# The chain to the MLP's factors in two parts: 56 tiles inside the drain of phase 1, the last 8 tiles on GpSimd in small pieces during phase 2

## The reference

```
ada = cond @ w_ada + b_ada                 # shift, scale, gate, twice
xm  = expmap0(layer_norm(logmap0(x)) * (1 + sc_msa) + sh_msa)
q, k, v = heads(plin(xm, w_q)), ...        # plin(x) = expmap0(logmap0(x) @ w + b)
z   = plin(attention(q, k, v), w_o)
x1  = mobius_add(x, expmap0(g_msa * logmap0(z)))      # = ALPHA * x + BETA * zg
xm  = expmap0(layer_norm(logmap0(x1)) * (1 + sc_mlp) + sh_mlp)
ff  = plin(plin(xm, w_f1), w_f2)
out = x + mobius_add(x1, expmap0(g_mlp * logmap0(ff)))
```

## Time and profile before

| | |
|---|---|
| median of 3 runs | 765.38 us (765.11 to 765.99) |
| the profiled execution | 765.7 us, its span 763.9 us |
| busy over the span | PE 644.4 us (84%), DVE 654.1 (86%), ACT 524.7 (69%), POOL 347.0 (45%) |
| 500 to 520 us | PE 0.00 us busy, DVE 16.86, ACT 6.57, POOL 2.57; granted clock 0.50 |
| 640 to 700 us | PE 57.26 us busy, DVE 56.25, ACT 55.22, POOL 23.58; granted clock 1.00 |

### The profile page before, as it was taken

How to read it: one execution, slowest core, us unless ns; L and a number is a source line. 1 busy time by engine, 2 the same in 40 slices (tenths; PEclk the granted TensorE clock), 3 DMA queues, 4 the chain that set the end, 5 groups by cost and what they waited for, 6 DMA issues and landing times. The chain is left out here.

```text
span 763.9 us, 27111 instructions
## 1 busy us (share of the span) xinstructions
PE 644.4 (84%) x8419; PEld 464.3 (61%) x8433; DVE 654.1 (86%) x2171; ACT 524.7 (69%) x1563; POOL 347.0 (45%) x683
## 2 busy tenths in 40 slices
PE   4956889999999999999999997605669999999996
PEld 2645667777777777777777775402326566656664
DVE  2786788999999999999999997485998999999975
ACT  1123567777777777777777775334879989999874
POOL 1003556666666666666666665111234244234321
PEclk9978899999999999999999998656999999999999
DMA  9942876666666666666666665222444455445523
GB/s 321 359 116 57 141 131 137 146 141 143 141 147 142 145 142 147 141 141 144 147 140 147 144 133 113 50 70 70 124 124 133 139 158 163 149 132 166 164 72 110
DMA packets 184804, 107.50 MB, mean 141 GB/s; under 512 B 140188, under 2 KB 167591, under 8 KB 184744
## 3 DMA queue, kind: packets, MB, share of 16 engines
q1 hardware_dynamic: 182952, 103.99, 55.6%
q10 hardware_dynamic: 1792, 2.89, 1.0%
HBM read 64.11 MB, written 9.18 MB: 96 GB/s over the span
## 5 line engine op out<-in xcount | busy, mean ns | idle before, releaser
L885 PE MATMUL p_qkv<-wqkv,tT 128*128 128x256 f32 x768 | 198.1, 396 | 5.5 <-DVE u L1143 5.5
L885 PEld LDWEIGHTS p_qkv<-wqkv,tT 128*128 128x128 f32 x768 | 139.7, 195 | 22.9 <-issue 6.3
L899 PEld LDWEIGHTS p_o<-v,pT 64*64 64x64 f32 x4096 | 66.7, 136 | 21.9 <-issue 21.9
L899 PE MATMUL p_o<-v,pT 64*64 64x17 f32 x4096 | 73.0, 210 | 0.0
L858 PE MATMUL p_oz<-wo,oT 128*128 128x256 f32 x256 | 69.7, 397 | 0.0
L445 POOL TENSOR_TENSOR rt<-ss_t,c_mhalf 128x1 f32<-128x1 f32 x64 | 42.1, 658 | 60.6 <-ACT junk L634 53.7
L659 ACT ACTIVATE pT<-p_s 128x1024 f32<-128x1024 f32 x64 | 65.6, 1024 | 2.8 <-PE p_s L875 1.7
L1143 DVE SCALAR_TENSOR_TENSOR u<-p_qkv,ct,bqkv 128x768 f32<-128x768 f32 x64 | 64.3, 1005 | 3.5 <-PE p_qkv L885 3.5
L617 ACT ACTIVATE oT<-p_oz 128x256 f32<-128x256 f32 x64 | 24.6, 384 | 57.0 <-PE p_oz L850 57.0
L504 POOL TENSOR_TENSOR rt<-ss,c_mhalf 128x2 f32<-128x2 f32 x32 | 26.5, 827 | 80.8 <-ACT wqkv L707 80.8
L933 PE MATMUL p_t<-ident,pT 128*128 128x128 f32 x128 | 21.3, 290 | 46.5 <-ACT pT L714 46.5
(11 more groups left out here) (275 smaller groups left out, 1685.2 us busy)
## 6 DMA issues: line engine op xcount, KB each, us to landing
mod<-mod_rows SPq DMA_DIRECT2D x128, 128.0 KB, 2.9
x_all<-in_x SPq DMA_DIRECT2D x8, 1024.0 KB, 14.3
gate<-mod_rows SPq DMA_DIRECT2D x128, 64.0 KB, 2.7
mod<-mod_rows SPq DMA_DIRECT2D x32, 256.0 KB, 4.2
mod_b<-mod_rows SPq DMA_DIRECT2D x32, 256.0 KB, 4.4
out<-x_all SPq DMA_DIRECT2D x32, 256.0 KB, 3.0
gate<-gate_rows SPq DMA_DIRECT2D x32, 128.0 KB, 2.9
bqkv<-gate_rows SPq DMA_DIRECT2D x32, 128.0 KB, 2.9
```

What stands on the lines that cost most here:

```text
L885: mm = pe.matmul(p_qkv[:, a * D:a * D + D], tT[:, k, c, :], wqkv[:, c, a * D:a * D + D], start=c == 0, stop=c == C - 1)
L899: mm = pe.matmul(p_o[S * e:S * e + S, col:col + VW], pT[keys, e, g, :], v[keys, k, 2 * g + e, :], start=True, stop=True, skip_group_check= ...
```

## The change

The chain's code is put into functions of ten stages, which work on a slice of the columns. EARLY are tiles 0 to 55, LATE are the last 8.

- EARLY: DVE runs the stages inside slots 64 to 69 of phase 1, between `dot_x` and `gate_z`; ACT answers in its slots 65 to 70, POOL computes the moments in slot 69. Only the two first sums, `log_map_norm`, `scale_t2` and `scale_of_norm` stay behind phase 1. `split_ff_bias` moves from slot 69 to slot 66.
- LATE: POOL does all of it in phase 2, in slots 2 to 24, each piece before (`late_middle`) or after (`late_end`) its `token_roots2`. [...] Inverse roots and reciprocals are powers there. ACT answers with one Tanh in slot 7 and one Ln in slot 20, the latter between two table loads. DVE and ACT wait for `late_made` before pair 28.
- SP's waits for phase 1 move into the slots of phase 2 that need them.

```diff
+        EARLY, LATE = slice(0, T - 2 * GROUP), slice(T - 2 * GROUP, T)
+        LATE_TANH, LATE_LN = 7, 20
@@ SP, slot2
+                    if i == 1:
+                        sp.wait_ge(o_psum, T)
...
+                    if i == 0:
+                        sp.wait_ge(zg_ready, T)
+                        sp.wait_ge(u_ready, T)
...
-            sp.wait_ge(zg_ready, T)
-            sp.wait_ge(u_ready, T)
-            sp.wait_ge(o_psum, T)
@@ POOL, phase 1 slot
+                if isinstance(h, int) and 2 * h + off == T + 5:
+                    moments_of_sum()
@@ POOL, slot2
                 if on2(h, off, M_B):
                     inner_roots(slots - M_B)
+                late_middle(slots)
                 if group_at(h, off, M_N) is not None:
                     output_roots(group_at(h, off, M_N), parity(off, M_N))
                 if on2(h, off, M_A):
                     token_roots2(slots - M_A)
                 if group_at(h, off, M_N) is not None:
                     norm_roots(group_at(h, off, M_N))
+                late_end(slots)
+            def fused(dst, a, s1, b, f1_, f2_):
+                step(pool.tensor_scalar(late_tmp[:, :], a, s1, None, f1_))
+                step(pool.tensor_tensor(row(dst), late_tmp[:, :], b, f2_))
+            def power(dst, a, exponent):
+                step(pool.tensor_tensor(row(dst), row(a), exponent[:, :], ALU.pow))
+            def late_middle(n):
...
+                if n == 13:
+                    tt(Y0, ALPHA, MEAN, ALU.mult)
+                    tt(Y1, BETA, ZMEAN, ALU.mult)
+                    tt(MEAN1, Y0, Y1, ALU.add)
+                    tt(Y0, AA, VAR, ALU.mult)
...
+                if n == 21:
+                    tt(W10, W10, W4, ALU.mult)
+                    pool.wait_ge(late_answers, 2)
+                    fused(W8, row(W8), 0.5, row(W4), ALU.mult, ALU.mult)
...
+            def late_end(n):
...
+                if n == 13:
+                    tt(Y1, BB, ZVAR, ALU.mult)
+                    tt(Y0, Y0, Y1, ALU.add)
+                    tt(Y1, AB2, COV, ALU.mult)
+                    tt(VAR1, Y0, Y1, ALU.add)
...
+                if n == 24:
+                    tt(R2, W12, W4, ALU.mult)
+                    pool.drain().then_inc(late_made, 1)
@@ ACT, phase 1 slot, after evac_tT and before square_z
+                if isinstance(h, int) and 2 * h + off in (T + 1, T + 2):
+                    cols[0] = EARLY
+                    rsq()
+                if isinstance(h, int) and 2 * h + off == T + 3:
+                    act.preload_act_table_set("exp_and_others")
+                    elementwise(ACT.Tanh, W7, W8)
+                if isinstance(h, int) and 2 * h + off == T + 5:
+                    act.preload_act_table_set("natural_log_exp_and_others")
+                    rsq()
+                if isinstance(h, int) and 2 * h + off == T + 6:
+                    elementwise(ACT.Ln, W7, W8)
@@ ACT, slot2, before square_ff
+                if slots == LATE_LN:
+                    act.wait_ge(late_asks, 2)
+                    act.preload_act_table_set("natural_log_exp_and_others")
+                    act.activation(row(W8), row(W7), ACT.Ln).then_inc(late_answers, 1)
+                    act.preload_act_table_set("exp_and_others")
@@ DVE, phase 1 slot, after dot_x and before gate_z
-                if isinstance(h, int) and 2 * h + off == T + L_L - 1:
-                    split_ff_bias()
+                if s == T:
+                    cols[0] = EARLY
+                    dve.wait_ge(stats_kept, EARLY.stop)
+                    moments_of_z()
+                if s == T + 1:
+                    clipped_z()
+                if s == T + 2:
+                    split_ff_bias()
+                    norm_of_z()
+                if s == T + 4:
+                    sum_factors()
+                    dve.drain().then_inc(alpha_made, 1)
+                    squared_factors()
+                    dve.drain().then_inc(sums_made, 1)
+                    norm_of_sum()
+                if s == T + 5:
+                    log_map_argument()
+                    log_map_series()
@@ DVE, between the phases
-            dve.wait_ge(stats_kept, T)
...
             for j in range(2):
                 first_sum(0, j)
-            log_map_argument()
-            log_map_series()
             dve.wait_ge(moment_step, 8)
             log_map_norm(VAR1)
```

More of the change, by code:

```diff
@@ L160, in build @@
         c_tiny = sb("c_tiny", [P, 1])
+        c_mone = sb("c_mone", [P, 8])
+        late_tmp = sb("late_tmp", [P, 8])
         ff = qk[:, :].rearrange("p (j d) -> p j d", j=2)
@@ L686, in scale_x @@
                 n = 2 * i + j
+                if n == LATE.start:
+                    act.wait_ge(late_made, 1)
                 after(act, x1_ready, n - 1)
@@ L689, in scale_x @@
                                scale=arrays[:, ALPHA, bass.ds(n, 1)]).then_inc(xa_ready, 1)
-            rsq()
-            rsq()
-            elementwise(ACT.Tanh, W7, W8)
-            act.preload_act_table_set("natural_log_exp_and_others")
             act.wait_ge(alpha_made, 1)
@@ L697, in _ @@
                 scale_x(0, j)
-            rsq()
-            elementwise(ACT.Ln, W7, W8)
             rsq()
@@ L773, in slot2 @@
                     tanh_norm(group_at(h, off, M_P))
+                if slots == LATE_TANH:
+                    cols[0] = LATE
+                    act.wait_ge(late_asks, 1)
+                    act.activation(row(W8), row(W7), ACT.Tanh).then_inc(late_answers, 1)
+                if slots == LATE_LN:
[3 more added lines that the diff above has]
+                    act.preload_act_table_set("exp_and_others")
                 if on2(h, off, M_B):
@@ L779, in slot2 @@
                         square_fg(slots - M_B, j, (off - M_B) % TURN, q, col)
-            act.preload_act_table(ACT.Tanh)
+            act.preload_act_table_set("exp_and_others")
             act.wait_ge(factors_made, 1)
@@ L1036, in take_rsq, with fused, reciprocal @@
                 stt(dst, W3, 1.5, W2_, ALU.add, ALU.mult)
-            def log_map_argument():
-                take_rsq(W4)
-                tt(W5, W0, W4, ALU.mult)
-                ts(W5, W5, MAX_ARG, ALU.min)
-                ts(W6, W5, -1.0, ALU.mult, 1.0, ALU.add)
-                step(dve.reciprocal(row(W6), row(W6)))
-                stt(W7, W5, 1.0, W6, ALU.add, ALU.mult)
-                ask()
-            def log_map_series():
-                tt(W9, W5, W5, ALU.mult)
-                ts(W10, W9, 1.0 / 15, ALU.mult)
-                for m in (13, 11, 9, 7, 5, 3):
-                    stt(W10, W10, 1.0 / m, W9, ALU.add, ALU.mult)
-                stt(W10, W10, 1.0, W5, ALU.add, ALU.mult)
-                tt(W10, W10, W4, ALU.mult)
-            def log_map_norm(var):
-                take()
-                stt(W8, W8, 0.5, W4, ALU.mult, ALU.mult)
-                tt(W10, W10, W8, ALU.subtract)
-                stt(W10, W5, SERIES_BELOW, W10, ALU.is_lt, ALU.mult)
-                tt(W12, W8, W10, ALU.add)
-                tt(W0, W12, W12, ALU.mult)
-                stt(W0, var, 0.0, W0, ALU.max, ALU.mult)
-                ts(W0, W0, LN_EPS, ALU.add)
-                ask()
-            def scale_of_norm(dst):
-                take_rsq(W4)
-                tt(dst, W12, W4, ALU.mult)
+            def fused(dst, a, s1, b, f1_, f2_):
+                step(dve.scalar_tensor_tensor(out=row(dst), in0=a, scalar=s1, in1=b, op0=f1_, op1=f2_))
+            def reciprocal(dst):
+                step(dve.reciprocal(row(dst), row(dst)))
+            (moments_of_z, clipped_z, norm_of_z, sum_factors, squared_factors, norm_of_sum, log_map_argument, log_map_series,
+             log_map_norm, scale_of_norm) = boundary_stages(dve, step, tt, ts, stt, fused, reciprocal, ask, take, take_rsq)
             def tile_of(big, i):
@@ L1472, in slot2 @@
                     half = (TURN // 2) * h + (off - M_A) // 2
+                    if 2 * i == LATE.start:
+                        dve.wait_ge(late_made, 1)
                     for j in range(2):
```

280 lines of the change are left out of this document (216 added, 64 removed).

## The result

The changed kernel takes 756.53 us (median of four runs, 755.44 to 757.36) beside 765.25 us for the one before (four runs); the ratio is 0.9888, 95% interval 0.9868 to 0.9909. 757.8 us was forecast. The profiled execution took 756.48 us, its span is 754.4 us, 9.5 us shorter than before.

What follows compares the result with a forecast made beforehand. PE and DVE are over 90% busy in both phases; the chain between them costs latency. 765.7 - 10.8 (boundary) + 2.5 (Ln) + 0.7 (DVE beside POOL) = 758.1, median 0.3 lower: 757.8 us, range 753.5 to 763.0.

Steps and rivals of the forecast that it cites:

- What is removed: Between the last `gate_z` and the first `shift_t2`: 23.8 us shrink to 6.7, so 17.1 us go.
- Slots 65 and 66: Drain: chain pieces and bias, 6.7 us, exceed 3.76 idle by 2.95; with 0.25 for slot 64, 3.2 us late.
- The clock at 480: Slot 67: PE's clock falls to half already at 480 us, its work taking 5.1 against 3.2 us: 1.9 us.
- Slot 68: Drain: `sum_factors` to `norm_of_sum` take 6.5 us; with the slower PE ahead, 1.2 us are over the idle time.
- Slot 69: Drain: `log_map_argument` and `log_map_series` take 5.0 us where the bias was; 1.9 us over.
- The drain: End of phase 1: delays of 3.2, 1.2 and 1.9 make it 6.3 us longer; phase 2 starts 10.8 us earlier.
- The Ln on ACT: Phase 2, slot 20: two table loads and an activation stop ACT 2.8 us; 2.5 us were taken as the cost.
- POOL's pieces: Phase 2: 87 small pieces at 0.35 us each lie hidden in POOL's gaps before rt and rh.
- DVE beside POOL: Phase 2: 81 POOL pieces slow DVE by 0.7 us in all, 5.4 us as upper bound.
- Rivals 2 and 3: Phase 2: POOL's pieces too long, 763 us (chance 0.13); POOL takes the port from DVE, 770 us (chance 0.08).
- rival 3: Phase 2: POOL takes DVE's port, 770 us; by the skill's rule 23 us held in all; chance 0.08.
- Its own signs of being wrong: First `shift_t2` far from 509.7 us, or a turn of four slots longer between slots 8 and 24 than after.

Runs made afterwards that it cites:

- run 5: The changed kernel with the bias split (`split_ff_bias`) moved from slot 66 to slot 2 of the start: 751.89 us, ratio 0.9828.
- run 1: The changed kernel without the logarithm of slot 20, both table loads gone and the Ln made a Copy: 752.44 us, ratio 0.9828.
- run 3: The changed kernel with nine unread matmuls on PE ahead of its wait in `transpose_t2` of slot 21: 754.36 us, ratio 0.986.
- run 4: The changed kernel with none of the late work on POOL and ACT in phase 2, six memsets standing in: 753.48 us, ratio 0.9831.
- run 12: The kernel before, unchanged, traced a second time: one execution, 765.75 us.
- run 11: The changed kernel with seven Copies on ACT in place of slot 20's Ln and its table loads: 756.22 us, ratio 0.9896.
- run 8: The kernel before with only the bias split moved to slot 2 of the start: 762.53 us, ratio 0.9972.
- run 2: The changed kernel with the second table load moved two slots behind the Ln: 754.86 us, ratio 0.986.

## Why the prediction was right, and where not

The sign and the time (757.8 for 756.5 us) were right, inside the likeliest case; two terms of the sum were off and a third thing wasn't in it. That the total came out so near is in part luck, as the last point shows.

- *What is removed*: 17.1 us forecast, 23.8 - 6.4, 17.5 with all digits, measured. Right.
- *Slots 65 and 66*: 3.2 us forecast. The `gate_z` of slot 66 stood 9.85 us behind the u of tile 63 before (468.56 and 478.41), and stands 12.66 behind it now (463.46 and 476.12): 2.8. Right, with no idle time before it; in run 5 it stands 10.46 behind.
- *The clock at 480*: half level in slot 67, right, and so its price, 2.0 us for the 1.9. PE waited 3.54 us ahead of it where 4.05 had been forecast. That it is the late `gate_z`, and PE's longer wait with it, that brings the clock down isn't shown: in run 5 the gate is 2.2 us earlier, PE waits 1.27 us, and the clock falls as well. Here the result fits the forecast, and the mechanism stays open.
- *Slot 68*: 6.5 us of chain forecast, 6.44 measured (484.52 to 490.96). *Slot 69*: 5.0 forecast, 5.4 measured (492.28 to 497.68).
- *The drain*: 6.3 us longer forecast; from the u of tile 63 to the last `gate_z` it took 28.08 us and takes 34.22, 6.1. The boundary gained 11.3 us for 10.8.
- *"The Ln on ACT ... I take 2.5"*: the mis-sized term. It cost 5.8. The sum went from one row, ACT's own time, which was right (2.81), and stopped there. Behind ACT PE had to wait 2.9 us, and came back at half clock for some 6 us. I had used just this step for slot 67 and left it out for slot 20. Runs 1 and 3 show the two halves, 2.8 and 3.0 us. The Trainium skill ("ScalarE: Activation LUTs", What ACT_TABLE_LOAD costs), with its 2.66 us a switch, would have given an estimate of 5.6 for the piece, near the 5.8, but by another way, a drain with each switch. The rows have no such drain, each activation starts 0.01 us behind its load, and in run 3 the piece costs 2.8 with both loads in it.
- *POOL's pieces*: hidden, right (run 4); from start to start 0.28 us, and 0.39 beside DVE's operations with two inputs from SBUF, for the forecast 0.35. *DVE beside POOL*: 0.7 us forecast, about 0.2 measured (0.02 to 0.1 a turn, run 4). Rivals 2 and 3 are out. The rule of the Trainium skill ("SBUF — State Buffer", SBUF: two separate sides), under which rival 3 had its worst case, isn't seen on DVE: its two-input operations keep to 475 to 484 ns, beside powers of 1.76 us too. On POOL the rows fit it, 0.32 us for a piece beside these operations and 0.21 elsewhere: if one engine waits there, it is POOL. That it waits for the port is not shown by itself.
- *Its own signs of being wrong*: the first `shift_t2` was to be near 509.7 us and came at 504.05. Of those 5.6 us the 5.1 below are phase 1's, so counted from the u of tile 63 the sum of the drain held. The turn of slots 21 to 24 was 6 us longer than the later ones, which was the sign for rivals 2 and 3; run 1 shows that it was the logarithm. And the low end of the forecast's own bounds, added up from the four terms, is 754.1 us and not 755.5.
- *Not in the sum*: the 5.1 us by which phase 1, untouched but for slot 64, was ahead in the trace. They hid the 3.3 us of the logarithm and 0.9 us in slots 2 to 9.

Those 5.1 us are a matter of single executions, at least in good part. Across the thirteen other traces, in code that is the same but for the bias split and slot 64, the u of tile 63 starts anywhere from 461.9 to 467.6 us, and slots 2 to 9 take 54.2 to 57.2 us where no matmuls are added. The start differs in single windows, as these, of the changed kernel and then of run 12, show:

```profile
85.00:90.00 5.00, 4.11 (x67) 1.00 0.68 142
```

```profile
85.00:90.00 5.00, 3.44 (x43) 0.66 1.00 126
```

The low window is not the old program's: run 11, of the new one, has 0.66 in it too.

What stays open: by the traces the change is worth 11.3 - 5.8 = 5.5 us (4.6 with the boundary of run 12), by the medians 8.7, with an interval of 7.0 to 10.1. The old program's two traces have tile 63 at 468.56 and 466.75 us, the seven of the new one without the early bias between 463.46 and 467.59, mean 465.2. A start of the old program that is 2 or 3 us slower on average would fit both, and chance in so few traces isn't excluded. The same holds for the 2 us of run 8. Nor did a run put SP's waits back, which the prediction took for free.

## What to carry to other kernels

Latency that lies between two phases can be put in the holes of the drain, if each piece is set against the idle time of its own slot: 17.5 us went from between the phases here, and 6.1 came back as a longer drain. A small chain on GpSimd costs next to nothing where each piece is shorter than the wait it lies in. But a stop of a few microseconds on an engine that feeds TensorE has to be priced at TensorE: ask how long it will wait, and add the half clock behind it (1.3 and 3.0 us behind two stops of the same length here); split such a stop in two, fill TensorE's wait ahead of it, or do the work without it. And where phase 1 of two traces differs in code that no one touched, compare between marks, not from zero.

## What the runs showed that I had not expected

- One wait of PE of 2.9 us in a phase where it is over 90% busy was followed by half clock for about 6 us (0.50 at 649 to 652, 0.59 at 652 to 655 us); the waits of run 2, at most 1.5 us long, were not. The length of one wait doesn't tell it alone: in the drain of run 5 half clock came behind a wait of 1.27 us, where PE had been busy for 0.7 of the 2 us before (474 to 476 us). With the clock up the same stop cost 2.8 instead of 5.8 us.
- Matmuls that nobody reads, 35 of them in the waits of four pairs, took 2.4 us out of eight slots (55.1 to 52.7, where the twelve traces without them have 54.2 to 57.2). Put behind a wait instead of ahead of it, such matmuls cost 5.9 us in the drain.
- GpSimd's products of 128x8 took 0.20 to 0.38 us and its operations with a scalar 0.20 to 0.49, so eight columns are hardly cheaper than 51. What made a piece long was DVE beside it: 0.32 against 0.21 us.
- The u of tile 63, behind some 460 us of code that is the same but for the bias split and slot 64, started up to 6.7 us earlier or later from one trace to another (461.9 and 468.56 us), and up to 4.1 us among the seven traces whose phase 1 is the same throughout (463.46 and 467.59).
